# Row order through DRAM: how a four-layer graph network spreads its softmax sums and exponent rows

## The chip, the cores and the metric

The kernel runs on one core of one Trainium2 chip. The metric is the device time of one execution in microseconds (us). The core has a matrix engine (PE), a vector engine (DVE), a scalar engine (ACT), GpSimd (POOL), and a queue engine (SP) that here only issues DMAs; 16 DMA engines carry them.

## The reference

32 graphs of 512 nodes with 256 channels share one 512x512 adjacency. Each graph passes four layers, each of the form `x = x + layer(relu(layernorm(x)))`:

```
L0: e = (h W1)(h W2)^T; e = leaky(e); mask by adj; softmax; relu(att @ (h W3))
L1: q = h W, 4 heads of 64;  e[i,j] = leaky(src[i] + dst[j]); mask; softmax; elu(att @ q)
L2: 4 heads of 64: softmax(mask(Q K^T / 8)) @ V, then Wo + bo, layernorm * gamma + beta
L3: as L1, with its own weights for each head
```

## The kernel before

Everything is float32. A graph is one "work"; its 512 nodes lie as 4 row blocks (`t`) on 128 partitions. The program is unrolled and has 33 turns ("slots"). In each turn an engine runs one list of steps, written out by hand, for up to three works at once: `a` enters (layer 0 and the front half of layer 1), `b` is the work before it (the back half of layer 1, then the scores of layer 2), and `c` the one before that (the back half of layer 2, then layer 3). The engines are in order and meet only at semaphores. Three sets of buffers rotate with the work's number.

Two things need a vector that lies across partitions turned into one that lies along the free axis on every partition.

**Exponent rows of the graph layers (g = 1 and 3).** ACT writes `grow` [128 partitions, 16 values] (L511). PE transposes it into PSUM (`gat_rows`, L1060), DVE copies that to `growT` [16, 128] (`gat_rows_out`, L736), and SP stores it to `r_dram` (L322), waits, and reads it back to all 128 partitions with two loads, into `qT` and `hT` (L326). DVE's weights of the graph layer, `gat_weights` (L753), read these rows. The first work's layer 1 and the last one's layer 3 get two of their four heads from PE instead.

**Inverse sums of the multi-head softmax (layer 2), in two pairs p of heads.** DVE takes the reciprocals `rinv` (`inverse_sums2`, L815). ACT spreads a pair's into [128, 512] (`inverse_columns`, L580), PE transposes that in four pieces (`inverse_spread`, L1126), and ACT copies the result out of PSUM (`inverse_out`, L588) to `kT`, which lies in the buffer `qx`. DVE multiplies the head outputs by it (`norm2`, L822). Only then can PE do the output projection `o_rows` (L972 on `wqkvo,qT`), whose result DVE takes in `o_out` (L829), the start of layer 2's own layernorm and of layer 3's.

Around the change PE's list is: head outputs of pair 0 (L1142), 24 transposes of softmax weights (L1115), the eight transposes of the inverse sums (L1126), head outputs of pair 1 (L1142), the first head of work b's layer 1 (`gat_aggregate(b, 1, 0)`, L1080), `o_rows(c, 0)`. ACT and DVE copy the transposed weights out of PSUM (L573, L806). Later, `transposed(c, 3, 0)` (L958) starts layer 3 on PE.

SP's list in a turn is: load the input of the next work (L301), spread the rows of work a's layer 1, store work c's output (L310), spread the rows of work b's layer 3. Since it is in order, each waits for those ahead of it:

```python
                spread(a, 1); store(c); spread(b, 3)
```

The entry for work b there is served in the turn in which the other engines call that work c.

Of the kernel before, what the change touches and what calls it, by code (L numbers as in the profile page):

```python
# [5 lines left out]
def gnn_stack_kernel(nc, x, adj, W1, W2, W3, gat1_W, gat1_a, Wq, bq, Wk, bk, Wv, bv, Wo, bo,  # L6
# [5 lines left out]
    f32 = mybir.dt.float32  # L12
# [5 lines left out]
    P = 128  # L18
# [8 lines left out]
    SETS = 3  # L27
# [8 lines left out]
    with ctx:  # L36
# [47 lines left out]
        growT = sets("growT", [H * NT, P])  # L84
# [11 lines left out]
        r_dram = {g: [nc.dram_tensor(f"r_dram{g}_{s}", [H * NT, P], f32).ap() for s in range(SETS)] for g in (1, 3)}  # L96
        prob2 = [[pA[s], pB[s], pX[0], pX[1]] for s in range(SETS)]
# [12 lines left out]
        def sem(name):  # L110
# [102 lines left out]
        rT_ready = per_gat("rT_ready")  # L213
        rT_out = per_gat("rT_out")
# [32 lines left out]
        invc_ready = Signal("invc_ready", 2)  # L247
        invp_ready = Signal("invp_ready", 2)
        inv_ready = Signal("inv_ready", 2)
# [46 lines left out]
        def _(sp):  # L296
# [19 lines left out]
            def spread(w, g):  # L316
# [4 lines left out]
                rT_out[g].wait(sp, w)  # L321
                sp.dma_start(rows_dram, growT[s][:, :]).then_inc(r_written[g].sem, 16)  # L322
# [116 lines left out]
        def _(act):  # L439
# [135 lines left out]
            def inverse_columns(w, p):  # L575

                if w is None:
                    return
                rinv2.wait(act, w, p + 1)
                nc.scalar.copy(kT[w.s][:, p, :].rearrange("p (t h d) -> p t h d", t=NT, h=2),  # L580
                               rinv[w.s][:, 2 * p:2 * p + 2, :].rearrange("p h t -> p t h").unsqueeze(3)
                               .broadcast_to([P, NT, 2, D])).then_inc(invc_ready.sem, 1)

            def inverse_out(w, p):
                if w is None:
                    return
                invp_ready.wait(act, w, p + 1)
                nc.scalar.copy(kT[w.s][:, p, :], ps[:, BANK[f"RB{p}"], :]).then_inc(inv_ready.sem, 1)  # L588
# [39 lines left out]
        def _(dve):  # L628
# [103 lines left out]
            def gat_rows_out(w, g):  # L732
                if w is None:
                    return
                rT_ready[g].wait(dve, w)
                nc.vector.tensor_copy(growT[w.s][:, :], ps[0:H * NT, BANK[f"RT{g}"], 0:P]).then_inc(rT_out[g].sem, 1)  # L736

# [79 lines left out]
            def norm2(w, p):  # L817
# [3 lines left out]
                inv_ready.wait(dve, w, p + 1)  # L821
# [19 lines left out]
            def slot(a, b, c, d):  # L841
                statistics(a, 0); inverse_sums2(c, 1); weights_out2(c, 2, 3); weights_out2(c, 3, 0)
                weights_out2(c, 3, 2); mean_and_variance(a, 0); gat_weights(b, 1, 0, 0, 1, 2, 3)
                norm2(c, 0); gat_weights(b, 1, 1, 0); shift_of_norm(a, 0); norm2(c, 1)
                gat_weights(b, 1, 1, 1, 2, 3); gat_weights(b, 1, 2, 0, 1, 2); o_out(c); statistics(c, "in")
# [7 lines left out]
                inverse_sum0(a); gat_shift(c, 3); weights_out0(a, 3); gat_rows_out(c, 3); statistics(a, 1)  # L853
# [11 lines left out]
                weights_out2(b, 0, 1); gat_shift(a, 1); gat_weights(c, 3, 3, 0, 1, 2); gat_rows_out(a, 1)  # L865
# [85 lines left out]
        def _(pe):  # L951
# [104 lines left out]
            def gat_rows(w, g):  # L1056
                if w is None:
                    return
# [3 lines left out]
                if lone(w, g) is None:  # L1062
                    return
# [244 lines left out]
```

## Time and profile before

| | |
|---|---|
| median of 3 runs | 2944.5 us (2943.93 to 2946.85) |
| profiled execution, span from first to last instruction | 2943.7 us (no time of its own is listed for it beside the span) |
| PE busy | 2887.3 us, 98% |
| DVE, ACT, POOL busy | 72%, 57%, 28% |
| mean granted PE clock | 0.997 |
| DMA | 109.89 MB, mean 37 GB/s |

The span is one profiled execution; it stands 0.8 us under the median. Busy time of PE is the union of its matmuls, whose ends are modelled, so 98% says that it is hardly ever without one in flight, not that it runs at its peak. In code and rows L is the line of the kernel before.

### The profile page before, as it was taken

The numbers are of one execution on the slowest core, as the hardware profiler recorded it, in microseconds if no ns is written. First come the engines' busy times: TensorE is split into PE (matmuls) and PEld (weight loads), VectorE is DVE, ScalarE is ACT, GpSimd is POOL, SyncE is SP. The second block draws the span as 40 slices with busy tenths as digits, with TensorE's granted clock in tenths as the row PEclk, the third lists the DMA queues.
The fourth block names the chain that finished last, engine by engine and source line by source line (L and its number), as shares of the span: only waits on it lengthen the run. The fifth ranks groups of instructions, "written<-read, shape, count | busy, mean of one in ns | idle before, by whom it ended". The sixth has DMA issues, their size and how long they took to land.

```text
span 2943.7 us, 68275 instructions
## 1 busy us (share of the span) xinstructions
PE 2887.3 (98%) x27732; PEld 2034.8 (69%) x27732; DVE 2127.5 (72%) x5596; ACT 1682.3 (57%) x3554; POOL 827.8 (28%) x917
## 2 busy tenths in 40 slices
PE   7899999999999999999999999999999999999998
PEld 5566767666767666767667767667767667776766
DVE  5576787776787776877776877776877777877764
ACT  2555655655656655656655656656656656656543
POOL 2123222323222323222233232233222233222221
PEclk9999999999999999999999999999999999999999
DMA  3001011101011101011101011101011111011010
GB/s 102 22 23 45 27 41 45 44 23 45 23 44 45 44 23 44 23 44 44 38 30 44 23 45 44 37 30 44 23 45 44 34 33 40 28 37 37 17 36 30
DMA packets 58840, 109.89 MB, mean 37 GB/s; under 512 B 5568, under 2 KB 41408, under 8 KB 58528
## 3 DMA queue, kind: packets, MB, share of 16 engines
q1 hardware_dynamic: 58032, 104.61, 10.8%
q8 instruction: 220, 3.60, 0.5%
q0 software_dynamic: 496, 0.92, 0.3%
q14 instruction: 92, 0.75, 0.1%
HBM read 88.21 MB, written 17.30 MB: 36 GB/s over the span
## 4 chain that ended last, share of the span: by engine, by line
PE 77%; DVE 12%; POOL 6%; issue 2%; ACT 1%; SPq 0%; DMA 0%; POOLq 0%; DVEq 0%; ACTq 0%
PE ps L972 19%; PE ps L1080 11%; PE ps L1106 8%; PE ps L1115 8%; PE ps L978 8%; PE ps L1142 8%; PE ps L1029 8%; PE ps L958 4%; DVE stats L641 3%; POOL rstd L367 3%; POOL xc L417 3%; DVE pB L753 2%; PE ps L1017 2%; DVE nb L658 1%; DVE hn L829 1%
## 5 line engine op out<-in xcount | busy, mean ns | idle before, releaser
L389 POOL TENSOR_TENSOR qx<-qx,xc 128x512 f32<-128x512 f32 x128 | 163.7, 1279 | 869.4 <-ACT qx L529 869.4
L641 DVE BATCH_NORM_STATS2 stats<-xc 128x6 f32<-128x256 f32 x384 | 134.7, 413 | 328.6 <-POOL xc L399 264.1
L448 ACT ACTIVATE hn<-xc,nb,rstd 128x256 f32<-128x256 f32 x384 | 209.1, 592 | 163.9 <-DVE nb L658 160.7
L1080 PEld LDWEIGHTS ps<-vals,pA 128*64 128x64 f32 x8192 | 253.9, 138 | 54.6 <-issue 54.5
L972 PE MATMUL ps<-wgat,hT 128*128 128x264 f32 x1024 | 267.4, 395 | 1.8 <-ACT hT L457 1.8
L1080 PE MATMUL ps<-vals,pA 128*64 128x65 f32 x8192 | 266.4, 223 | 2.1 <-DVE pA L753 2.0
L1080 PE MATMUL ps<-vals,pB 128*64 128x65 f32 x8192 | 264.0, 223 | 0.3 <-DVE pB L753 0.2
L1080 PEld LDWEIGHTS ps<-vals,pB 128*64 128x64 f32 x8192 | 249.7, 138 | 16.8 <-issue 16.7
L457 ACT COPY hT<-ps 128x1024 f32<-128x1024 f32 x128 | 129.7, 1013 | 224.0 <-PE ps L958 219.8
L1106 PE MATMUL ps<-qx,qT 64*128 64x512 f32 x1024 | 249.8, 614 | 1.1 <-DVE hn L767 0.8
L364 POOL TENSOR_SCALAR rstd<-mv 128x4 f32<-128x4 f32 x160 | 75.0, 469 | 610.2 <-DVE mv L650 610.2
L1029 PE MATMUL ps<-vals,pB 128*128 128x256 f32 x1024 | 243.2, 381 | 1.1 <-ACT vals L469 1.1
L1142 PE MATMUL ps<-pX,vals 128*64 128x512 f32 x512 | 233.6, 599 | 2.3 <-DVE pA L806 2.3
L978 PE MATMUL ps<-hT,wqkvo 128*128 128x512 f32 x512 | 233.0, 598 | 0.8 <-ACT hT L457 0.8
L1008 PE MATMUL ps<-hT,qT 128*128 128x512 f32 x512 | 228.3, 599 | 1.1 <-ACT qT L463 1.1
L1029 PEld LDWEIGHTS ps<-vals,pB 128*128 128x128 f32 x1024 | 190.6, 191 | 38.9 <-issue 14.8
L972 PEld LDWEIGHTS ps<-wgat,hT 128*128 128x128 f32 x1024 | 179.5, 190 | 50.4 <-issue 24.9
L958 PE MATMUL ps<-ident,hn 128*128 128x128 f32 x1024 | 199.0, 280 | 11.9 <-ACT hn L448 11.1
L958 PEld LDWEIGHTS ps<-ident,hn 128*128 128x128 f32 x1024 | 132.3, 141 | 105.3 <-DVE rowmax L667 32.7
L367 POOL TENSOR_TENSOR rstd<-rstd,minus_half 128x4 f32<-128x4 f32 x160 | 192.5, 1203 | 13.3
L753 DVE SCALAR_TENSOR_TENSOR pA<-qT,gval,adjT 128x512 f32<-128x512 f32 x248 | 184.5, 785 | 6.7 <-DMA hT<-r_dram 6.5
L562 ACT ACTIVATE pX<-pX,negmax 128x512 f32<-128x512 f32 x256 | 183.4, 720 | 0.6 <-DVE negmax L797 0.6
(147 smaller groups left out, 6194.3 us busy)
## 6 DMA issues: line engine op xcount, KB each, us to landing
qT<-r_dram SPq DMA_DIRECT2D x64, 512.0 KB, 3.9
hT<-r_dram SPq DMA_DIRECT2D x64, 512.0 KB, 4.9
x_in<-in_x SPq DMA_DIRECT2D x32, 512.0 KB, 3.9
out_x<-xc SPq DMA_DIRECT2D x32, 512.0 KB, 3.0
pX<-in_adj SPq DMA_DIRECT2D x1, 1024.0 KB, 8.1
r_dram<-growT SPq DMA_DIRECT2D x64, 8.0 KB, 1.3
pX<-in_L_gnn_W SPq DMA_DIRECT2D x2, 256.0 KB, 5.2
pA<-in_L_gnn_a POOLq DMA_DIRECT2D x8, 64.0 KB, 8.8
```

Source lines behind the costliest of these rows:

```text
L367: nc.gpsimd.tensor_tensor(rstd[s][:, :], rstd[s][:, :], minus_half[:, :], ALU.pow).then_inc(rstd_ready[norm].sem, 1)
L641: last = nc.vector.bn_stats(stats[s][:, t, :], src[:, t, :])
L753: last = nc.vector.scalar_tensor_tensor(out=gat_p[s][h % 2][:, t, :], in0=row, scalar=gval[s][:, 1, t, h:h + 1], in1=adjT[:, t, :], op0=AL ...
L958: last = nc.tensor.transpose(ps[:, bank + k, t * P:(t + 1) * P], hn[s][:, t, k * P:(k + 1) * P], ident[:, :])
L972: last = nc.tensor.matmul(at, src[w.s][:, k, t * P:(t + 1) * P], wt[:, k, 0:width], start=(k == 0), stop=(k == KT - 1))
L978: last = nc.tensor.matmul(ps[:, bank + m, :], wt[:, k, m * P:(m + 1) * P], hT[w.s][:, k, :], start=(k == 0), stop=(k == KT - 1))
L1008: last = nc.tensor.matmul(ps[:, BANK[f"E{t}"], :], qT[s][:, k, t * P:(t + 1) * P], hT[s][:, k, :], start=(k == 0), stop=(k == KT - 1))
L1029: last = nc.tensor.matmul(rows_in(BANK["A"])[:, t, :], pB[s][:, t, j * P:(j + 1) * P], vals[s][:, j, 0:C], start=(j == 0), stop=(j == NT - 1))
L1080: last = nc.tensor.matmul(ps[lo:hi, BANK[f"G{g}.{h}"], t * DV:(t + 1) * DV], gat_p[s][h % 2][:, j, t * P + lo:t * P + hi], vals[s][:, j, h ...
L1106: last = nc.tensor.matmul(ps[:, BANK[f"S{p}.{t}"] + hh, :], qT[s][at, p, t * P:(t + 1) * P], kT[s][at, p, :], start=True, stop=True)
L1115: last = nc.tensor.transpose(ps[:, BANK[f"PT{h}.{t}"], j * P:(j + 1) * P], prob2[w.s][h][:, t, j * P:(j + 1) * P], ident[:, :])
L1142: last = nc.tensor.matmul(ps[hh * D:(hh + 1) * D, BANK[f"G2.{p}"], :], vals[s][:, j, h * D:(h + 1) * D], probT2[s][h][:, :, j * P:(j + 1) ...
```

## The change

Both vectors now go to DRAM directly from their partition layout. The destination is written in row order: for each of the 128 partitions its 16 values (`grow`) or 8 values (one pair of `rinv`) go to addresses that lie 128 elements apart. The access pattern's last dimension is therefore one element of 4 bytes. They are read back spread: the exponent rows as before, the inverse sums of one pair in two loads of 64 partitions each. The transposes for them on PE, the copies on ACT (L580, L588) and DVE (L736), one PSUM wait of PE (`rT_out`) and `growT` go. SP's list gets two new steps in each turn, and on DVE the second `norm2` stands one `gat_weights` instruction later.

```diff
+        inv_dram = [nc.dram_tensor(f"inv_dram_{s}", [2, 2 * NT, P], f32).ap() for s in range(SETS)]
...
-                rT_out[g].wait(sp, w)
-                sp.dma_start(rows_dram, growT[s][:, :]).then_inc(r_written[g].sem, 16)
+                grow_ready[g].wait(sp, w)
+                sp.dma_start(rows_dram.rearrange("m p -> p m"), grow[s][:, :, :].rearrange("p h t -> p (h t)"),
+                             allow_slow_non_contiguous=True).then_inc(r_written[g].sem, 16)
                 r_written[g].wait(sp, w, 16)
...
+            def inverse_spread(w, p):
+
+                if w is None:
+                    return
+                s, rows_dram = w.s, inv_dram[w.s][p]
+                rinv2.wait(sp, w, p + 1)
+                sp.dma_start(rows_dram.rearrange("m p -> p m"),
+                             rinv[s][:, 2 * p:2 * p + 2, :].rearrange("p h t -> p (h t)"),
+                             allow_slow_non_contiguous=True).then_inc(inv_written[p].sem, 16)
+                inv_written[p].wait(sp, w, 16)
+                for hh in range(2):
+                    src = rows_dram.rearrange("(o h t) p -> o h (t p)", o=1, h=2)[:, hh, :]
+                    sp.dma_start(kT[s][hh * D:(hh + 1) * D, p, :],
+                                 src.broadcast_to([D, N])).then_inc(inv_loaded[p].sem, 16)
...
-                spread(a, 1); store(c); spread(b, 3)
+                inverse_spread(b, 0); spread(a, 1); store(c); inverse_spread(b, 1); spread(b, 3)
...
-                inv_ready.wait(dve, w, p + 1)
+                inv_loaded[p].wait(dve, w, 32)
...
-                norm2(c, 0); gat_weights(b, 1, 1, 0); shift_of_norm(a, 0); norm2(c, 1)
-                gat_weights(b, 1, 1, 1, 2, 3); gat_weights(b, 1, 2, 0, 1, 2); o_out(c); statistics(c, "in")
+                norm2(c, 0); gat_weights(b, 1, 1, 0); shift_of_norm(a, 0); gat_weights(b, 1, 1, 1)
+                norm2(c, 1); gat_weights(b, 1, 1, 2, 3); gat_weights(b, 1, 2, 0, 1, 2); o_out(c); statistics(c, "in")
...
-                pT2_act[2].wait(pe, c, 2); weights_transposed2(c, 3, 3); inverse_spread(c, 0)
-                pT2_dve[2].wait(pe, c, 2); inverse_spread(c, 1); aggregate2(c, 1); gat_aggregate(b, 1, 0)
+                pT2_act[2].wait(pe, c, 2); weights_transposed2(c, 3, 3)
+                pT2_dve[2].wait(pe, c, 2); aggregate2(c, 1); gat_aggregate(b, 1, 0)
```

SP's DMAs in one turn, before. The first `r_dram` is the rows of layer 1 and the second those of layer 3; each is followed by its two loads.

```order
L301 DMA x_in<-in_x 128x4x256
L322 DMA r_dram_2<-growT 16x128
L326 DMA qT<-r_dram_2 128x1024
L326 DMA hT<-r_dram_2 128x1024
L310 DMA out_x<-xc 128x4x256
L322 DMA r_dram_1<-growT 16x128
L326 DMA qT<-r_dram_1 128x1024
L326 DMA hT<-r_dram_1 128x1024
```

The same turn on SP after the change, with the changed kernel's line numbers.

```order
L298 DMA x_in<-in_x 128x4x256
L332 DMA inv_dram<-rinv 128x8x1
L338 DMA qx<-inv_dram 64x512 x2
L319 DMA r_dram_2<-grow 128x16x1
L324 DMA qT<-r_dram_2 128x1024
L324 DMA hT<-r_dram_2 128x1024
L307 DMA out_x<-xc 128x4x256
L332 DMA inv_dram<-rinv 128x8x1
L338 DMA qx<-inv_dram 64x512 x2
L319 DMA r_dram_1<-grow 128x16x1
L324 DMA qT<-r_dram_1 128x1024
L324 DMA hT<-r_dram_1 128x1024
```

The store and the two loads of the first pair of inverse sums now stand ahead of layer 1's rows, and those of the second pair behind the output's store. Both kinds of store have one-element rows (x1).

On PE, the place between the head outputs of the two pairs, before.

```order
L1142 MATMUL ps<-pX,vals 64x512
L1142 MATMUL ps<-pA,vals 64x512
L1115 MATMUL ps<-ident,pX 128x128 x24
L1126 MATMUL ps<-ident,qx 128x128 x8
L1142 MATMUL ps<-pB,vals 64x512
L1142 MATMUL ps<-pX,vals 64x512
```

And after.

```order
L1120 MATMUL ps<-pX,vals 64x512
L1120 MATMUL ps<-pA,vals 64x512
L1103 MATMUL ps<-ident,pX 128x128 x24
L1120 MATMUL ps<-pB,vals 64x512
L1120 MATMUL ps<-pX,vals 64x512
```

The eight transposes of the inverse sums are gone, so that the head outputs of pair 1 stand directly behind the last transposes of the weights that they use.

On DVE, the two `norm2` (they write `qT` from `ps` and `qx`) among work b's `gat_weights`, before.

```order
L753 SCALAR_TENSOR_TENSOR pA<-qT,gval,adjT 128x512 x4
L822 TENSOR_TENSOR qT<-ps,qx 128x512
L753 SCALAR_TENSOR_TENSOR pB<-qT,gval,adjT 128x512
L658 SCALAR_TENSOR_TENSOR nb<-mv,rstd 128x4
L822 TENSOR_TENSOR qT<-ps,qx 128x512
L753 SCALAR_TENSOR_TENSOR pB<-qT,gval,adjT 128x512 x3
```

And after.

```order
L745 SCALAR_TENSOR_TENSOR pA<-qT,gval,adjT 128x512 x4
L814 TENSOR_TENSOR qT<-ps,qx 128x512
L745 SCALAR_TENSOR_TENSOR pB<-qT,gval,adjT 128x512
L656 SCALAR_TENSOR_TENSOR nb<-mv,rstd 128x4
L745 SCALAR_TENSOR_TENSOR pB<-qT,gval,adjT 128x512
L814 TENSOR_TENSOR qT<-ps,qx 128x512
```

The second `norm2` stands behind one more `gat_weights` instruction.

## Rows read from the trace of the kernel before

**Rows 1.** The page: the chain that ended last, share of the span by engine.

```profile
PE 77%; DVE 12%; POOL 6%; issue 2%; ACT 1%; SPq 0%; DMA 0%; POOLq 0%; DVEq 0%; ACTq 0%
```

**Rows 2.** One turn's two stretches: busy PE, PEld, DVE, ACT, POOL; granted clock, DMA.

```profile
1413.80:1484.50 70.70, 70.58 (x634) 51.06 (x634) 50.72 (x134) 44.95 (x99) 17.45 (x21) 1.00 0.13 46
1484.50:1502.50 18.00, 17.71 (x223) 10.96 (x222) 15.25 (x41) 7.56 (x13) 8.21 (x7) 1.00 0.01 2
```

**Rows 3.** Timeline of PE: start, length, operation; in brackets idle before, releaser.

```profile
1413.82 0.41 PE L958 MATMUL ps<-ident,hn 128*128 128x128 f32 x2 [0.28 <-ACT hn L448]
...
1480.15 1.13 PE L972 MATMUL ps<-wqkvo,qT 128*128 128x256 f32 x4
...
1502.50 0.41 PE L958 MATMUL ps<-ident,hn 128*128 128x128 f32 x2 [0.29 <-ACT hn L448]
```

**Rows 4.** The chain that ended last, pieces in order of time.

```profile
1463.35 0.11 PE ps L1060
...
1470.78 2.77 PE ps L1115 x24
1473.55 0.44 PE ps L1126 x4
```

**Rows 5.** Timeline around the transposes of the inverse sums, ACT and PE.

```profile
1472.77 0.59 ACT L573 COPY pX<-ps 128x512 f32<-128x512 f32 x1 [0.34 <-PE ps L1115]
...
1473.77 0.59 ACT L573 COPY pX<-ps 128x512 f32<-128x512 f32 x1
...
1474.70 0.61 PE L1142 MATMUL ps<-pB,vals 128*64 128x512 f32 x1
```

**Rows 6.** Timeline of DVE, from the inverse sums of pair 1 to `o_out`.

```profile
1472.07 0.18 DVE L815 RECIPROCAL rinv<-rowsum 128x8 f32<-128x8 f32 x1
...
1474.37 2.70 DVE L753 SCALAR_TENSOR_TENSOR pA<-qT,gval,adjT 128x512 f32<-128x512 f32 x4
1476.99 0.68 DVE L822 TENSOR_TENSOR qT<-ps,qx 128x512 f32<-128x512 f32 x1
...
1478.39 0.69 DVE L822 TENSOR_TENSOR qT<-ps,qx 128x512 f32<-128x512 f32 x1
1479.00 2.07 DVE L753 SCALAR_TENSOR_TENSOR pB<-qT,gval,adjT 128x512 f32<-128x512 f32 x3
...
1484.57 1.23 DVE L829 TENSOR_TENSOR hn<-ps,b_rows 128x1024 f32<-128x1024 f32 x1 [1.52 <-PE ps L972]
```

**Rows 7.** Timeline of SP's DMA issues, layer 3's rows, then layer 1's and the output's store.

```profile
1428.19 0.32 SPq L322 DMA_DIRECT2D r_dram<-growT  x1
1429.55 0.32 SPq L326 DMA_DIRECT2D qT<-r_dram  x1
1429.91 0.43 SPq L326 DMA_DIRECT2D hT<-r_dram  x1
...
1463.81 0.32 SPq L322 DMA_DIRECT2D r_dram<-growT  x1
1465.66 0.32 SPq L326 DMA_DIRECT2D qT<-r_dram  x1
...
1470.87 0.39 SPq L310 DMA_DIRECT2D out_x<-xc  x1
```

**Rows 8.** Timeline: the inverse sums of pair 0 and the exponent rows.

```profile
1460.33 0.18 DVE L815 RECIPROCAL rinv<-rowsum 128x8 f32<-128x8 f32 x1
...
1462.14 0.24 ACT L511 ACTIVATE grow<-gexp 128x16 f32<-128x16 f32 x1
```

**Rows 9.** DMA issues: count, KB each, median us to landing; page, then 1462 to 1476 us.

```profile
hT<-r_dram SPq DMA_DIRECT2D x64, 512.0 KB, 4.9
out_x<-xc SPq DMA_DIRECT2D x32, 512.0 KB, 3.0
...
hT<-r_dram SPq DMA_DIRECT2D x1, 512.0 KB, 6.5
```

**Rows 10.** DMA packets in 10.3 to 10.8 us, while the small weight blocks load.

```profile
DMA packets 482, 0.14 MB, mean 283 GB/s; under 512 B 453, under 2 KB 482, under 8 KB 482
```

More of the change, by code:

```diff
@@ L83, in gnn_stack_kernel @@
         grow = sets("grow", [P, H, NT])
-        growT = sets("growT", [H * NT, P])
         pX = [sb(f"pX{n}", [P, NT, N]) for n in range(3)]
@@ L246, in gnn_stack_kernel @@
         rinv2 = Signal("rinv2", 2)
-        invc_ready = Signal("invc_ready", 2)
-        invp_ready = Signal("invp_ready", 2)
-        inv_ready = Signal("inv_ready", 2)
+        inv_written = [Signal(f"inv_written{p}", 16) for p in range(2)]
+        inv_loaded = [Signal(f"inv_loaded{p}", 32) for p in range(2)]
         agg2_ready = Signal("agg2_ready", 2)
@@ L573, in weights_out2 @@
                 nc.scalar.copy(probT2[w.s][h][:, t, :], ps[:, BANK[f"PT{h}.{t}"], :]).then_inc(pT2_act[h].sem, 1)
[L575 to L588, printed above, removed]
             def slot(a, b, c, d):
-                inverse_columns(c, 0); exp2(c, 3, 3); gat_exp(b, 1); weights_out2(c, 2, 2)
-                weights_out2(c, 3, 1); inverse_columns(c, 1); weights_out2(c, 3, 3); inverse_out(c, 0)
-                inverse_out(c, 1); normalised(a, 0, 0); normalised(a, 0, 1); normalised(a, 0, 2)
+                exp2(c, 3, 3); gat_exp(b, 1); weights_out2(c, 2, 2)
+                weights_out2(c, 3, 1); weights_out2(c, 3, 3)
+                normalised(a, 0, 0); normalised(a, 0, 1); normalised(a, 0, 2)
                 normalised(a, 0, 3); h_transposed(a, 0); normalised(c, "in", 0); normalised(c, "in", 1)
@@ L730, in gat_shift @@
                                         ALU.mult, ALU.min).then_inc(gexp_ready[g].sem, 1)
[L732 to L736, printed above, removed]
             def gat_weights(w, g, h, *ts):
@@ L864, in slot @@
                 gat_norm(c, 3, 1); gat_max(a, 1); weights_out2(b, 1, 0); inverse_sums2(b, 0)
-                weights_out2(b, 0, 1); gat_shift(a, 1); gat_weights(c, 3, 3, 0, 1, 2); gat_rows_out(a, 1)
+                weights_out2(b, 0, 1); gat_shift(a, 1); gat_weights(c, 3, 3, 0, 1, 2)
                 gat_weights(c, 3, 3, 3); weights_out2(b, 0, 3); weights_out2(b, 2, 1); weights_out2(b, 1, 2)
@@ L943, in first @@
                 mean_and_variance(a, 1); shift_of_norm(a, 1); poison(); adjacency_out(); gat_max_t(a, 1)
-                gat_max(a, 1); gat_shift(a, 1); gat_rows_out(a, 1)
+                gat_max(a, 1); gat_shift(a, 1)
                 dve.wait_ge(setup_ok, SETUP)
@@ L1056, in gat_rows @@
             def gat_rows(w, g):
-                if w is None:
+                if w is None or lone(w, g) is None:
                     return
                 grow_ready[g].wait(pe, w)
-                nc.tensor.transpose(ps[0:H * NT, BANK[f"RT{g}"], 0:P], grow[w.s][:, :, :].rearrange("p h t -> p (h t)"),
-                                    ident[:, :]).then_inc(rT_ready[g].sem, 1)
-                if lone(w, g) is None:
-                    return
                 for h in range(2):
@@ L1117, in weights_transposed2 @@
                 last.then_inc(pT2p_ready[h].sem, 1)
-            def inverse_spread(w, p):
-                if w is None:
-                    return
-                invc_ready.wait(pe, w, p + 1)
-                for t in range(NT):
-                    cols = slice(t * P, (t + 1) * P)
-                    last = nc.tensor.transpose(ps[:, BANK[f"RB{p}"], cols], kT[w.s][:, p, cols], ident[:, :])
-                last.then_inc(invp_ready.sem, 1)
             def aggregate2(w, p):
@@ L1192, in slot @@
                 agg0_norm.wait(pe, a, 4); v_rows(b, 2, 0); scores2(b, 0, 0); scores2(b, 1, 0)
-                rT_out[3].wait(pe, c); scores2(b, 0, 1)
+                scores2(b, 0, 1)
                 masked2[0].wait(pe, b, 2); scores2(b, 0, 2); v_rows(b, 2, 1)
```

4 lines of the change are left out of this document (1 added, 3 removed), and 4 rows, old and new, of the table BANK.

## The prediction

> **What bounds the kernel now.** The chain that ended last comes first: 77% of it is PE, and DVE and POOL have 18% [rows 1]. So PE is the bound for most of the span but not for all of it, and one must ask where. The stretches show it: a turn is 88.7 us long, 70.7 us of it from the first transpose of layer 3 (L958) to the end of the output projection, and 18.0 us from there to the same transpose of the next turn [rows 2]. At the end of the second stretch PE sits idle for 0.28 us until ACT delivers `hn`, in this turn and in the next [rows 3]: those 18.0 us are a chain from `o_out` over two layernorms on DVE, POOL and ACT, and PE's work in it is cover. In the 70.7 us PE works without a break. A microsecond taken from PE in the first stretch moves `o_rows` and everything behind it; nothing that the change touches lies in the second. All 88.7 us turns are alike, and 32 of the 33 have the steps that the change touches, so I work in times of the turn around 1413.8 to 1502.5 us and multiply by 32. The sum is made against the span of 2943.7 us; the median of the runs is 0.8 us above it, and I put the difference on the median.
>
> **What the change takes from PE.** The transpose of the exponent rows costs PE 0.11 us, twice in a turn (L1060, the one at 1463.35 stands for both) [rows 4]. Both stand in the first stretch, with PE work ready behind them: 0.22 us.
>
> The eight transposes of the inverse sums begin at 1473.55 [rows 4] and the head outputs of pair 1 (L1142) at 1474.70 [rows 5], so they take 1.15 us. But this is not what goes. L1142 needs the last block of weights, which PE has transposed by 1473.55 and which ACT copies from 1473.77 to 1474.36 [rows 5]. Today the eight transposes hide that copy. Without them ACT, which no longer has L580 ahead, starts it as it started the one before: that block was complete after 16 of the 24 transposes, at 1470.78 + 16 x 0.115 = 1472.63, and ACT began at 1472.77, 0.14 us later [rows 4, 5]. So the copy runs from 1473.69 to 1474.28, and with about 0.12 us for the semaphore PE starts at 1474.40, 0.30 us earlier than now. PE will stand idle there for 0.85 us of the 1.15. The sum is 0.22 + 0.30 = 0.52 us in a turn, and 32 x 0.52 = 16.6 us.
>
> The copies taken from ACT (L580, L588) and DVE (L736) lie beside other work and give nothing more. On DVE the second `norm2` ran from 1478.39 to 1479.07 [rows 6]; one `gat_weights` (2.07 / 3, 0.67 us between starts) later and some 0.2 us earlier through PE's lead it ends at about 1479.5. PE reaches `o_rows` at 1480.15 - 0.52 = 1479.63 [rows 3]. This just fits, with 0.1 us to spare. Behind it DVE waits 1.52 us for `o_out` anyway [rows 6].
>
> **What it adds: one-element rows.** The store of exponent rows becomes 128 x 16 = 2048 pieces of 4 bytes, 128 for each of the 16 DMA engines; that of a pair of inverse sums 1024 pieces, 64 for each. Today's store has one piece for each engine, and the load that waits for it is issued 1.36 us after it [rows 7]. The price e of one such piece is shown nowhere. From below it is nothing. From above, a general bound: the output's store has 32 pieces of 1 KB for each engine and lands in 3.0 us [rows 9], (3.0 - 1.33) / 31 = 54 ns. The nearest row is that of the weight blocks: 482 packets, 453 of them under 512 bytes, in 0.5 us on 16 engines [rows 10], 30 for each engine, which is 16.6 ns a packet, in a stretch in which the engines had work throughout. Those were 256-byte loads. A 4-byte piece has less to move but the same fixed part, so I take e = 12 ns. A store with n pieces for each engine then takes 1.33 us + n e from its issue to the load's issue: 2.9 us for the exponent rows, 2.1 us for a pair of sums.
>
> The Trainium skill ("DMA: Bandwidth & Descriptors", "Rules for kernel authors") says that a strided last dimension lowers to one descriptor per element and advises against it. The same page ("Specifications") says that below 512 bytes the DMA engine does a read-modify-write. For the loads of [rows 10] the trace shows no such penalty; for stores of 4 bytes no row here can show it. By that rule e would be the third rival's below.
>
> **Where the new steps wait.** SP is in order, so I follow it.
> - Pair 0: the sums are there at 1460.51 [rows 8]. Store at 1460.6, its loads at 1461.93 + 0.064 e, SP free again 0.72 us later (two issues, 0.36 us apart as in [rows 7]) at 1462.65 + 0.064 e, e in ns. The exponent rows have been there since 1462.38 [rows 8]; before, SP got them at 1463.81 over PE and DVE [rows 7].
> - Exponent rows of layer 1: the two small loads ahead in the DMA engines cost some 0.6 us (an estimate, 256 KB at half the time of the 512 KB load's data), so the big loads go out at 1464.6 + 0.192 e. With e = 12 that is 1466.9, against 1465.66 today [rows 7], 1.2 us later. `hT` is issued 0.36 us behind and lands after 4.9 us in the median and 6.5 in this turn [rows 9]: 1472.2 to 1473.8. DVE reads it at 1474.37 [rows 6], or 0.2 us earlier. It stays hidden, for e up to 14 in the worst turns and 21 in the median.
> - Output's store: free to go at 1470.87 as today [rows 7], its data behind what is left of the big loads.
> - Pair 1: sums at 1472.25 [rows 6]. Its store is queued in the DMA engines behind the output's. The data of the big loads end about 0.7 us before they land, the output's data need 1.6 us, the pieces 0.064 e, 0.25 us for SP, then two loads of 64 x 2 KB. Their landing lies between 1.33 us and the 3.0 us of the output's 512 KB; I take 2.6, and 0.36 for the second issue. With 0.7 us of `norm2` and its semaphore, `o_rows` can start at 1475.7 + 0.256 e in an average turn (0.8 later in this one). With e = 12 that is 1478.8, against the 1479.63 at which PE comes.
> - Layer 3's rows: their store also skips the hop over PE and DVE, which for layer 1 took 1463.81 - 1462.38 = 1.4 us, and pays 128 e = 1.5 us. The loads go out when they do now.
>
> So the gain is whole up to e = 15, zero at e = 17.4 (`o_rows` at 1480.15), and each nanosecond above costs 0.256 x 32 = 8.2 us. What waits behind it: on SP layer 3's rows, on DVE the rest of work b's `gat_weights`, on PE everything.
>
> **Forecast: 2944.5 - 16.6 = 2928 us**, and 2918 to 2937 for this case alone (0.8 us of gain at most, 0.25 at least).
>
> **Rivals.**
> 1. *The pieces are as slow as big ones; slower.* With e = 30 `o_rows` starts at 1483.4, 3.2 us late: 2944.5 + 104 = 3049. With the bound of 54 it starts at 1489.5: +300, 3245. It decides at e = 17.4, only 5 ns above my value. For it: nothing shows a 4-byte store, and 16.6 ns would already take all the gain. Against it: packets got cheaper with size wherever rows show both. Chance 0.29 with all values of e from 18.5 up, without the next.
> 2. *No change.* e between 16 and 18.5, or `norm2`, one instruction later, taking the gain with its 0.1 us of room. 2940 to 2950, chance 0.11.
> 3. *Each piece is a read and a write.* As a mechanism of this kernel: each store piece costs two small packets, 2 x 16.6 = 33 ns, `o_rows` at 1484.2, 4.0 x 32 = +128: 3072. Chance 0.10. This is the read-modify-write of the Trainium skill's page named above.
> 4. *All 1.15 us go.* If the last copy were not awaited, 1.37 us a turn and 2901 us. Against it speaks the copy's end at 1474.36, and DVE's `norm2` at 1479.5, which then binds. Chance 0.03.
>
> The forecast's own case keeps 0.47. A measurement of this kernel tells about 0.2% (6 us) from no change. Faster: 0.47 + 0.03 = 0.50; same 0.11; slower 0.39. Range: 2918 leaves out rival 4; the upper end of 3110 is e = 37 and leaves out the part above, about 0.17.
>
> **What would show it.** Right: L1060 and L1126 gone, PE idle for some 0.85 us ahead of L1142, the turn 88.2 us, `norm2` without a wait for a DMA, the stores landing in 2 to 3 us. Wrong: DVE L822 or L753 released by DMAs from `inv_dram` or `r_dram`, a gap on PE in front of `o_rows`, stores of more than 3.6 us. If PE's gaps grow the granted clock may fall as well, which I do not price.

## The result, and the profile after

| | before | after |
|---|---|---|
| median | 2944.3 us (2943.93 to 2946.85, 4 runs) | 3829.1 us (3827.78 to 3830.52, 4 runs) |
| span of the profiled execution | 2943.7 us | 3827.3 us |
| mean granted PE clock | 0.997 | 0.903 |
| packets under 512 bytes | 5,568 | 205,249 |

The ratio is 1.300, with a 95% interval of 1.298 to 1.302. The median is far outside the range of 2918 to 3110, and on the other side of the forecast. The extra 885 us are spread over all turns: the one that I followed is 116.6 us long instead of 88.7, and 32 times these 27.9 us are 893.

The page of the changed kernel: busy time of each engine, granted clock in 40 slices, packets, and the chain that ended last by engine and by line.

```profile
PE 3087.2 (81%) x27412; PEld 2169.4 (57%) x27412; DVE 2106.7 (55%) x5532; ACT 1621.1 (42%) x3426; POOL 795.4 (21%) x917
...
PEclk9898898998888998988998988988899988899988
...
DMA packets 265687, 126.91 MB, mean 33 GB/s; under 512 B 205249, under 2 KB 240065, under 8 KB 265377
...
DMA 42%; PE 26%; DVE 16%; issue 6%; POOL 5%; SPq 3%; ACT 2%; POOLq 0%; DVEq 0%; ACTq 0%
DMA r_dram<-grow 17%; DMA inv_dram<-rinv 17%; PE ps L964 14%; DMA hT<-r_dram 5%; PE ps L1094 4%; PE ps L950 3%; DMA qx<-inv_dram 3%; DVE pB L745 2%; DVE pA L745 2%; POOL rstd L380 2%; DVE stats L639 2%; POOL xc L430 2%; PE ps L1021 2%; DVE pX L779 2%; PE ps L1068 2%
```

Where PE had 77% of the chain [rows 1], DMAs have 42% now, and the two new kinds of store alone 34%. PE waits for what hangs behind them. The waits of PE, then those of SP: what was waited for, us in total, times, longest. "issue" is time in which the engine waited for nothing that the profile shows.

```profile
PE ps L1068 <- DVE pA L745: 287.5, 34, 14.5
PE ps L964 <- DVE qT L814: 198.7, 32, 8.3
PE ps L1068 <- issue: 89.6, 57, 4.6
PE ps L1094 <- DVE rowmax L779: 78.7, 31, 4.4
...
SPq L324 <- DMA r_dram<-grow: 629.4, 64, 10.9
SPq L338 <- DMA inv_dram<-rinv: 616.6, 56, 14.5
```

SP waits 629.4 / 64 = 9.8 us for a store of rows and 616.6 / 56 = 11.0 us for one of sums. Its timeline through one turn shows the order: pair 0's sums, work a's rows, the output, pair 1's sums.

```profile
1884.01 0.37 SPq L332 DMA_DIRECT2D inv_dram<-rinv  x1
1893.57 1.10 SPq L338 DMA_DIRECT2D qx<-inv_dram  x2
1894.71 0.59 SPq L319 DMA_DIRECT2D r_dram<-grow  x1
1904.15 0.34 SPq L324 DMA_DIRECT2D qT<-r_dram  x1
...
1905.01 0.43 SPq L307 DMA_DIRECT2D out_x<-xc  x1
1905.49 0.61 SPq L332 DMA_DIRECT2D inv_dram<-rinv  x1
1919.52 1.09 SPq L338 DMA_DIRECT2D qx<-inv_dram  x2
```

From a store's issue to the next issue it takes 9.56 us for pair 0, 9.44 for the rows and 14.03 for pair 1, which has the output's store ahead of it. I had 2.1 and 2.9 for the first two. The load for the rows leaves 1904.15 - 1884.01 = 20.1 us after pair 0's store, instead of 1466.9 - 1460.6 = 6.3. Who waits at the end, on DVE and then on PE:

```profile
1911.59 2.74 DVE L745 SCALAR_TENSOR_TENSOR pA<-qT,gval,adjT 128x512 f32<-128x512 f32 x4 [8.83 <-DMA hT<-r_dram]
...
1923.34 0.69 DVE L814 TENSOR_TENSOR qT<-ps,qx 128x512 f32<-128x512 f32 x1 [7.02 <-DMA qx<-inv_dram]
...
1914.47 3.72 PE L1068 MATMUL ps<-vals,pA 128*64 128x65 f32 x64 [8.09 <-DVE pA L745]
1924.09 2.07 PE L964 MATMUL ps<-wqkvo,qT 128*128 128x256 f32 x4 [5.89 <-DVE qT L814]
```

Work b's weights wait 8.83 us for the rows, `norm2` of pair 1 waits 7.02 us for its sums, and PE stands 8.09 and then 5.89 us. In this turn the 64 matmuls behind the first wait take 3.72 us; 64 of the same form take 2.09 us at 1937.18, where PE had not stopped. The windows view of a later turn shows the clock behind such a wait at 0.67, a mixture of its two levels, 1.2 and 2.4 GHz (busy times, clock, DMA share, GB/s):

```profile
2031.00:2041.00 10.00, 3.46 (x64) 3.35 (x64) 2.21 (x5) 2.08 (x4) 0.00 (x0) 0.67 0.14 28
```

The rows of layer 3 are late in the same way. Their store is issued at 1847.50 and the loads behind it at 1857.85, 10.35 us later instead of 1.36 [rows 7], and DVE waits for them:

```profile
1863.17 0.75 DVE L745 SCALAR_TENSOR_TENSOR pA<-qT,gval,adjT 128x512 f32<-128x512 f32 x1 [3.34 <-DMA hT<-r_dram]
```

DVE's row maxima of work b (`rowmax`) stand behind these weights in its list, and PE's 78.7 us are the wait for them.

What takes the 10 us is not the pieces. The DMA view of 1848 to 1858 us, in 40 slices of 0.25 us, shows one store of rows that was issued at 1847.50, and nothing else but 16 packets (the first row is the busy share of the 16 DMA engines in tenths):

```profile
DMA  0077776000000000000000000000000000000000
...
DMA packets 2064, 0.01 MB, mean 1 GB/s; under 512 B 2064, under 2 KB 2064, under 8 KB 2064
```

The 2048 pieces pass within five slices, 1.25 us, or 1.25 / 128 = 9.8 ns for each on an engine. I had put e at 12 ns. They are gone at 1849.75, the load that waits for them is issued at 1857.85, and in those 8.1 us no packet of any DMA passes. One piece for each element is what the Trainium skill says of a strided last dimension ("DMA: Bandwidth & Descriptors", "Rules for kernel authors"); the 2,064 packets agree. The same page ("Anatomy of one DMA") says, of DMAs that GpSimd issues, that the fixed part is mostly the receipt of the last write, and that it can be surprisingly long into HBM; it has about 2 us. The 8.1 us of this trace, on SP's queue, lie in the same place, behind the last piece; that they are such a receipt no row shows.

### The profile page after: what moved, and what is told of

The parts are those of the page before. It is cut to its first block, busy times and chain, and to the rows that moved or that the text cites. A ratio compares the mean times of both kernels' runs of the same rounds, so it can differ in the third digit from the quotient of the medians.

```text
span 3827.3 us, 67603 instructions
## 1 busy us (share of the span) xinstructions
PE 3087.2 (81%) x27412; PEld 2169.4 (57%) x27412; DVE 2106.7 (55%) x5532; ACT 1621.1 (42%) x3426; POOL 795.4 (21%) x917
## 2 busy tenths in 40 slices
DMA packets 265687, 126.91 MB, mean 33 GB/s; under 512 B 205249, under 2 KB 240065, under 8 KB 265377
## 4 chain that ended last, share of the span: by engine, by line
DMA 42%; PE 26%; DVE 16%; issue 6%; POOL 5%; SPq 3%; ACT 2%; POOLq 0%; DVEq 0%; ACTq 0%
DMA r_dram<-grow 17%; DMA inv_dram<-rinv 17%; PE ps L964 14%; DMA hT<-r_dram 5%; PE ps L1094 4%; PE ps L950 3%; DMA qx<-inv_dram 3%; DVE pB L745 2%; DVE pA L745 2%; POOL rstd L380 2%; DVE stats L639 2%; POOL xc L430 2%; PE ps L1021 2%; DVE pX L779 2%; PE ps L1068 2%
## 5 line engine op out<-in xcount | busy, mean ns | idle before, releaser
L1068 PE MATMUL ps<-vals,pA 128*64 128x65 f32 x8192 | 317.5, 246 | 287.5 <-DVE pA L745 287.5
L1068 PEld LDWEIGHTS ps<-vals,pA 128*64 128x64 f32 x8192 | 299.6, 159 | 349.0 <-issue 348.1
L1068 PE MATMUL ps<-vals,pB 128*64 128x65 f32 x8192 | 295.7, 228 | 91.3 <-issue 89.6
L964 PE MATMUL ps<-wqkvo,qT 128*128 128x256 f32 x512 | 197.8, 529 | 198.7 <-DVE qT L814 198.7
L1068 PEld LDWEIGHTS ps<-vals,pB 128*64 128x64 f32 x8192 | 272.1, 142 | 115.6 <-issue 113.6
L1094 PE MATMUL ps<-qx,qT 64*128 64x512 f32 x1024 | 267.4, 640 | 79.7 <-DVE rowmax L779 78.7
L377 POOL TENSOR_SCALAR rstd<-mv 128x4 f32<-128x4 f32 x160 | 52.8, 330 | 1262.8 <-DVE mv L648 1262.8
L1120 PE MATMUL ps<-pX,vals 128*64 128x512 f32 x512 | 255.0, 644 | 2.2 <-ACT pA L586 1.7
L964 PEld LDWEIGHTS ps<-wqkvo,qT 128*128 128x128 f32 x512 | 127.7, 275 | 222.6 <-DVE qT L814 205.1
L461 ACT ACTIVATE hn<-x_in,nb,rstd 128x256 f32<-128x256 f32 x128 | 66.4, 589 | 435.3 <-DVE nb L656 435.3
```

What stands on the lines that cost most here:

```text
L461: nc.scalar.activation(hn[s][:, t, :], src[:, t, :], ACT.Identity if norm == "in" else ACT.Relu, bias=nb[s][:, t:t + 1], scale=rstd[s][:, ...
L964: last = nc.tensor.matmul(at, src[w.s][:, k, t * P:(t + 1) * P], wt[:, k, 0:width], start=(k == 0), stop=(k == KT - 1))
L1068: last = nc.tensor.matmul(ps[lo:hi, BANK[f"G{g}.{h}"], t * DV:(t + 1) * DV], gat_p[s][h % 2][:, j, t * P + lo:t * P + hi], vals[s][:, j, h ...
L1094: last = nc.tensor.matmul(ps[:, BANK[f"S{p}.{t}"] + hh, :], qT[s][at, p, t * P:(t + 1) * P], kT[s][at, p, :], start=True, stop=True)
L1120: last = nc.tensor.matmul(ps[hh * D:(hh + 1) * D, BANK[f"G2.{p}"], :], vals[s][:, j, h * D:(h + 1) * D], probT2[s][h][:, :, j * P:(j + 1) ...
```

## The experiments

All are compared with the kernel before, whose median was 2945.1 to 2946.0 us beside them. The first four divide the change.

**Rows alone.** The kernel before, with only the exponent rows stored in pieces:

```diff
-                rT_out[g].wait(sp, w)
-                sp.dma_start(rows_dram, growT[s][:, :]).then_inc(r_written[g].sem, 16)
+                grow_ready[g].wait(sp, w)
+                sp.dma_start(rows_dram.rearrange("m p -> p m"), grow[s][:, :, :].rearrange("p h t -> p (h t)"),
+                             allow_slow_non_contiguous=True).then_inc(r_written[g].sem, 16)
```

> One part alone: only the exponent rows go to DRAM in 4-byte pieces; the inverse sums keep the kernel before's path over ACT and PE. In the changed kernel such a store takes 9.4 to 10.4 us from its issue to the issue of the load behind it, against 1.36. Theory A (the stores' long completion is what costs, each where it is awaited): layer 3's rows come about 7.9 us later less the 1.4 us hop, DVE waits some 3.5 us; layer 1's come 6.5 us later against 1.9 of slack, 4.6 us; together with PE's slower clock behind the gaps 8 to 12 us a turn, so 3200 to 3330 us. Rival (the two parts only hurt together, because SP is in order and the pair-0 step stands ahead of the rows): under 3 us a turn, below 3040 us.

**Sums alone.** The changed kernel, with the rows over PE and DVE again (that diff the other way round) and one semaphore `inv_written` for both pairs.

> The other part alone: only the inverse sums go to DRAM in 4-byte pieces, in the order of the changed kernel on SP; the exponent rows keep the path over PE. Theory A: SP waits 9.6 us for pair 0 (1460.6 to 1470.2 in the turn of the kernel before), layer 1's rows are stored then instead of at 1463.81, 6.4 us late against a slack of 1.9 to 3.5 us; pair 1 is stored behind the output and completes 14 us after its issue, so o_rows starts some 8 to 13 us late: 12 to 16 us a turn in all, 3330 to 3460 us. If this and the run with the rows alone add up to the 885 us of the whole change, the parts are independent; if they add to clearly less, they hurt more together. Rival as there: under 3 us a turn.

Measured: 3284.8 us for the rows alone (ratio 1.1145, 1.1123 to 1.1167), 3472.9 us for the sums alone (1.1784, 1.1766 to 1.1802). That is +340 and +528, together 868, where the whole change has +885. So neither half needs the other to cost. The first lies in its expected range, the second 13 us above it. PE's waits, of the rows alone and then of the sums alone:

```profile
PE ps L1105 <- DVE rowmax L788: 103.9, 31, 4.4
PE ps L1079 <- issue: 57.5, 91, 2.8
```

```profile
PE ps L972 <- DVE qT L822: 258.8, 32, 9.4
PE ps L1080 <- issue: 86.6, 43, 3.4
```

Each half has its own wait and also one that is released by nothing ("issue"). With the rows alone PE's longest wait in sum is the one behind layer 3's rows (`rowmax`, 103.9 us), with the sums alone the one behind `norm2`.

**Wide pieces.** The changed kernel, with both stores in the order of the partitions, 64 or 32 bytes in a piece; every instruction and wait stays. It leaves out the turn into row order, so that rows and sums come back permuted and the kernel computes something else in the same steps.

```diff
-                sp.dma_start(rows_dram.rearrange("m p -> p m"), grow[s]...
+                sp.dma_start(rows_dram.rearrange("m p -> (m p)").rearrange("(p m) -> p m", p=P), grow[s]...
```

> The changed kernel with both stores written in partition order, so that each partition's 16 or 8 values are one piece of 64 or 32 bytes; they are read back in the wrong order, so the values of rows and sums are permuted, and all instructions, waits and queues are those of the change. Theory A: the stores complete in about 1.5 us, nothing waits for them, and only the gain of the prediction is left, 0.52 us a turn: 2928 us (2920 to 2940). Rival (the cost lies in SP's order, in the loads of the sums or in the bare number of DMAs, not in the one-element pieces): stays above 3000 us.

Measured: 2934.1 us, ratio 0.9960 (0.9947 to 0.9972). All 895 us between the two are thus the layout of the two stores. The page (KB each, median us to landing) and PE's timeline ahead of pair 1:

```profile
PE 2847.4 (97%) x27412; PEld 2003.3 (68%) x27412; DVE 2110.8 (72%) x5532; ACT 1620.3 (55%) x3426; POOL 826.6 (28%) x917
...
r_dram<-grow SPq DMA_DIRECT2D x64, 8.0 KB, 2.0
inv_dram<-rinv SPq DMA_DIRECT2D x64, 4.0 KB, 1.7
```

```profile
1465.46 0.61 PE L1120 MATMUL ps<-pB,vals 128*64 128x512 f32 x1 [0.88 <-ACT pX L586]
```

The stores land in 2.0 and 1.7 us, and PE waits 0.88 us for ACT's last copy. Against this kernel, which has the same instructions, the 894.9 us of the changed one's span divide: PE is busy 3087.2 - 2847.4 = 239.8 us longer with the same 27,412 matmuls (the clock), and idle 655.1 us longer. The four rows of its waits above sum to 654.5, and the same four come to 3.8 us in all with wide pieces.

**The probe.** The kernel before, with two tests and a marker store in each turn, in SP's idle stretch behind the input's load. Nobody reads them, and SP alone waits for them, one after another, so that its waits price each form.

```diff
+            sp.dma_start(dst, src, allow_slow_non_contiguous=True).then_inc(probe_sem, 16)
+            probes[0] += 16
+            sp.wait_ge(probe_sem, probes[0])
...
+        PROBES = [("vals_sixteen", "load"), ("vals_eight", "apart_sixteen"), ("vals_four", "apart_row"),
+                  ("vals_one", "apart_two"), ("major", "apart_four"), ("gap", "apart_eight"),
+                  ("pair", "sbuf"), ("oct", "wide")]
```

> The kernel before, plus stores that nobody reads: in each turn, in SP's idle stretch behind the input's load, two test DMAs from a constant tile and a plain marker (16 pieces of 512 bytes), each awaited by SP alone, so that the next issue shows how long it took. 16 forms. Row order with 16, 8, 4 and 1 values for each partition; 16 values with neighbouring partitions 2, 4, 8, 16 and 128 elements apart in DRAM; partition order in pieces of 64 bytes, 4 bytes with gaps, 512 bytes; pieces of 8 and 32 bytes in row order; one-element pieces into SBUF; a one-element load. Theory A1 (pieces that fall into the same 64 bytes of DRAM wait for each other, 16 x 0.5 us): row order 9.5 us whatever the number of values, 5.5, 3.5 and 2.5 us at 2, 4 and 8 apart, 2.7 us at 16 and 128 apart, 8 bytes wide 5.3 us, 32 bytes wide 2 us. Theory A2 (any store of pieces below 64 bytes has one fixed tail of 8 us): 9 to 10 us for every form with 4-byte pieces into DRAM, wherever they fall. Theory A3 (each piece costs its engine a fixed time): 9.5 us for 16 values, 5 for 8, 1.8 for 1. For all of them SBUF as the target is 2 to 3 us. If PE's instruction supply suffers from such stores, PE shows gaps of 1 us and more released by nothing also here, although no engine waits for a store; if not, the whole stays at 2944.

**The probe, second place.** In the first place the input's load, a few microseconds earlier, still ran ahead of the test. So the kinds that had stood there stood second, behind a small marker store.

> The probe again, with the marker first and each form second, so that the input's 512 KB load, which stood right ahead of the first place, no longer weighs on it. Forms: row order with 16, 8, 4 and 1 values for each partition; 16 values in partition order with gaps; 64-byte pieces; 8-byte and 32-byte pieces in row order. In the first probe the first place cost some 2 us more than the second (12.3, 11.0, 10.0, 8.2, 12.5, 3.7, 6.3 and 3.7 us in this order of forms). Theory A1 as modified by the first probe (a chain of pieces in the same 64 bytes, 0.3 to 0.45 us for each, on a base of 1.5 to 4.5 us): 10, 9, 8, 6, 10, 1.6, 4 and 1.6 us; 32-byte and 64-byte pieces cost as little as 512-byte ones although they are no longer. Rival (the load ahead is not what differs): the same times as in the first place.

The second places of both, as SP's waits (total, times, longest), the second probe first. The names end in the number of values for each partition, or in the distance of the pieces in elements of 4 bytes; `gap` has 16 values for each partition 8 bytes apart, `pair` pieces of 8 bytes, `oct` of 32, `major` of 64, `wide` of 512, and `pr` is the same source into SBUF.

```profile
SPq L205 <- DMA pdvals_sixteen<-ident: 40.4, 4, 10.6
SPq L205 <- DMA pdgap<-ident: 36.0, 4, 10.1
...
SPq L205 <- DMA pdvals_one<-ident: 26.7, 4, 6.9
SPq L205 <- DMA pdpair<-ident: 12.0, 3, 4.1
SPq L205 <- DMA pdmajor<-ident: 4.6, 4, 1.4
SPq L205 <- DMA pdoct<-ident: 4.0, 3, 1.6
```

```profile
SPq L205 <- DMA pdapart_two<-ident: 29.2, 4, 7.8
SPq L205 <- DMA pdapart_four<-ident: 21.0, 4, 5.6
SPq L205 <- DMA pdapart_sixteen<-ident: 18.8, 4, 5.5
...
SPq L205 <- DMA pdapart_eight<-ident: 17.6, 4, 4.7
...
SPq L205 <- DMA pr<-ident: 7.6, 3, 3.0
SPq L205 <- DMA pdwide<-ident: 3.6, 3, 1.2
```

Per store SP waits 10.1 us (the issue itself, some 0.4 us, is not in it) for 2048 packed pieces and still 6.7 for 128: a sixteenth of the pieces saves a third. The same 2048 pieces take 4.4 to 4.7 us where they lie 32 or 64 bytes apart, and 2.5 us in SBUF. Pieces of 32 and 64 bytes take 1.2 to 1.3 us, and those of 512 bytes 1.2. So the wait follows how closely small pieces lie together in DRAM far more than their number. Two rows say that distance is not all. At 8 bytes from piece to piece, pieces of 4 bytes take 7.3 us in row order (`apart_two`), 9.0 where the neighbours come from one partition (`gap`), and pieces of 8 bytes only 4.0 (`pair`). Of the expected theories none holds whole: A2 fails by the pieces that lie apart, A3 by the 128 pieces, and A1 has the right order of the forms, but too little for pieces 64 bytes apart (2.7 us from issue to issue, where some 5 were measured). The kernels with the probes took 2945.6 and 2943.7 us, one run each: in this place on SP the stores cost nothing that shows. The Trainium skill says that the DMA engine does a read-modify-write below 512 bytes ("DMA: Bandwidth & Descriptors", "Specifications"); at 32 and 64 bytes these rows show no penalty against 512.

**Overlapped.** The changed kernel, with SP issuing pair 0's store and the rows' store before it waits for either.

```diff
-                inverse_spread(b, 0); spread(a, 1); store(c); inverse_spread(b, 1); spread(b, 3)
+                inverse_spread(b, 0); spread(a, 1); spread_back(a, 1); inverse_back(b, 0); store(c)
+                inverse_spread(b, 1); inverse_back(b, 1); spread(b, 3); spread_back(b, 3)
```

> The changed kernel with SP's waits moved: the store of pair 0 and that of layer 1's rows are both issued before either is awaited, so that their completions run side by side; nothing else differs. Theory A (each 4-byte store has a long completion, and SP, in order, puts one behind the other): layer 1's rows are stored right when they are there instead of 9 to 10 us later, so DVE's wait for them (8.8 us in a turn of the changed kernel) falls by 3 to 6 us and the turn of 116.6 us to 110 to 114: 3620 to 3750 us. Rival (stores in flight together hold each other up and take as long as one after the other): 3800 us and more.

Measured: 3752.4 us, ratio 1.2738 (1.2720 to 1.2755), 77 us less than the changed kernel and less of a gain than expected. PE's waits and SP's:

```profile
PE ps L1079 <- issue: 131.2, 119, 4.7
PE ps L1079 <- DVE pA L756: 91.2, 33, 12.5
...
SPq L329 <- DMA r_dram<-grow: 779.0, 63, 16.7
SPq L348 <- DMA inv_dram<-rinv: 388.9, 33, 13.8
```

The wait for layer 1's rows fell from 287.5 to 91.2 us as intended, but SP's waits for the two kinds of store are still 779.0 + 388.9 = 1167.9 us, where one after the other they were 629.4 + 616.6 = 1246.0. In one turn the loads for layer 1's rows leave 1870.0 - 1853.5 = 16.5 us after pair 0's store, instead of 20.1. Side by side the two take nearly as long as in turn, and the gaps that nothing releases grew from 89.6 to 131.2 us.

**Unread.** The kernel before, with one store of 1024 packed pieces in each turn, at pair 0's place, which nobody reads and SP awaits only in the next turn. No step waits for it.

```diff
+                rinv2.wait(sp, w, 1)
+                sp.dma_start(unread_dram.rearrange("m p -> p m"), ident[:, 0:8],
+                             allow_slow_non_contiguous=True).then_inc(w12_in, 16)
...
-                spread(a, 1); store(c); spread(b, 3)
+                unread(b); spread(a, 1); store(c); spread(b, 3)
```

> The kernel before, with one extra store of 1024 4-byte pieces from a constant tile in each turn, issued where the changed kernel issues that of pair 0 (when its sums are ready, ahead of the rows of layer 1), read by nobody and awaited only a turn later. It tells apart what a 4-byte store does to others. Theory S (it holds up what comes after it in the DMA engines and the instruction supply): PE shows gaps of 1 us and more released by nothing inside the aggregations of layer 3, 2 to 3 us a turn, and the plain 512-byte store of the rows behind it completes late, 5 to 9 us after its issue instead of 1.4 to 1.9, which its slack of 1.9 to 3.5 us does not cover: 3 to 8 us a turn, 3040 to 3200 us. Rival (only those who wait for the 4-byte store pay, and PE's gaps in the changed kernel come from its own late start): 2945 us within 6.

Measured: 3077.1 us, ratio 1.0441 (1.0425 to 1.0457): +131 us for 32 stores that nobody awaits. PE's waits, SP's timeline and PE's:

```profile
PE ps L1091 <- issue: 75.6, 50, 3.3
...
1525.18 0.37 SPq L334 DMA_DIRECT2D unread<-ident  x1
1528.45 0.32 SPq L324 DMA_DIRECT2D r_dram<-growT  x1
1534.28 0.33 SPq L328 DMA_DIRECT2D qT<-r_dram  x1
...
1532.48 0.22 PE L1091 MATMUL ps<-vals,pB 128*64 128x65 f32 x1 [1.78 <-issue]
```

The plain store of the rows behind it, 512 bytes in a piece, takes 5.83 us instead of 1.36 to 1.85 [rows 7]. Over all turns SP's timeline has 5.6 to 7.7 us for it. The Trainium skill says that the semaphore's increment lands only after every earlier write of that DMA engine ("DMA: Bandwidth & Descriptors", "Queues, rings and completion order"), which agrees: the load behind the plain store leaves 9.1 us after the unread one was issued, and in the probe a store of 1024 packed pieces takes 8.8 us and its issue. And PE stops among its small matmuls (64 of them in 2.09 us, 0.03 us apart) with nothing to wait for. In 28 of the 32 turns a gap of over 0.5 us begins 5.5 to 6.6 us after the issue of the unread store.

**Unread, two controls.** The same number of stores at the same place: in the order of the partitions (pieces of 32 bytes), and with the same 1024 pieces of 4 bytes, but 64 bytes apart.

```diff
-                sp.dma_start(unread_dram.rearrange("m p -> p m"), ident[:, 0:8],
+                sp.dma_start(unread_dram.rearrange("m p -> (m p)").rearrange("(p m) -> p m", p=P), ident[:, 0:8],
```

```diff
-        unread_dram = nc.dram_tensor("unread", [8, P], f32).ap()
+        unread_dram = nc.dram_tensor("unread", [8, P, 16], f32).ap()[:, :, 0]
```

> Control of the unread store: same place, same bytes, same number of partitions, but each partition's 8 values as one 32-byte piece. Theory S (4-byte pieces in the same 64 bytes of DRAM hold up the DMA engines, and PE's instructions with them): no gaps on PE, the rows' store behind it in 1.4 to 2.5 us, 2945 us within 6. Rival (any extra store at this place does it): 3077 us again.

> The unread store with its 1024 pieces of 4 bytes 64 bytes apart, so that no two fall into the same 64 bytes; number and size of the pieces are those of the unread store. In the probe this form took 4.6 to 5.3 us with 2048 pieces, against 8.3 to 10.8 us for 1024 packed ones. If sharing 64 bytes is what holds things up: gaps on PE shrink to under half (75.6 us in all before) and the kernel takes 2945 to 2990 us. If the small size alone does it: 3050 us and more.

Measured: 2945.5 us for both, ratios 0.9998 (0.9989 to 1.0007) and 1.0001 (0.9992 to 1.0011), and PE's waits list no such gap. The plain store behind takes 1.35 to 3.7 us there. The last one's page and the unread kernel's have the same row of packets, but for the mean rate; this is the one 64 bytes apart:

```profile
DMA packets 92121, 110.03 MB, mean 37 GB/s; under 512 B 38848, under 2 KB 74688, under 8 KB 91808
```

So 92,121 packets cost nothing here and 131 us when 1024 of each turn's are packed. Neither the size nor the number of the pieces does it.

**Two hops.** The kernel before, with pair 0 and layer 3's rows off PE but without packed pieces: a store in the order of the partitions, a load of single elements that turns it, a store of 512-byte rows, the spread loads.

```diff
+                sp.dma_start(flat, src).then_inc(hop.sem, 16)
+                hop.wait(sp, w, at + 16)
+                sp.dma_start(dst[:, :], flat.rearrange("p m -> m p"),
+                             allow_slow_non_contiguous=True).then_inc(hop.sem, 16)
```

> A version without any 4-byte store: pair 0's sums and layer 3's rows, the two with the most time, go to DRAM in partition order (pieces of 32 and 64 bytes), come back as 8 or 16 rows with a one-element load (3.4 us in the probe), are stored in 512-byte rows and spread as before. Layer 1's rows and pair 1 keep PE. PE loses one transpose of rows and four of sums in a turn. Theory: every hop stays hidden (pair 0 has 16 us until its use, layer 3's rows arrive 3 us later than before against 3.7 of slack); of the wide-piece version's 0.40 us a turn some 0.2 to 0.3 remain: 2935 to 2940 us. Rival (a hop is not hidden, most likely layer 3's rows in the turns in which instruction loads interfere): 2945 to 2970 us.

Measured: 2948.9 us, ratio 1.0012 (1.0003 to 1.0020), so not the gain I expected. Its page has 172,761 packets, 115,136 of them under 512 bytes, and costs 3 us for them: single-element loads don't do what packed stores do. The time lies in the range of the expected rival, a hop that isn't hidden. A turn is 88.48 us long (88.58 before), but PE waits 14.9 us in all for ACT's copy of pair 1's sums, and the turns at both ends are longer. I didn't follow that further.

**Columns early.** The gain side of the forecast says that PE hides ACT's last copy. So I moved one step of the kernel before, on ACT, out of that copy's way:

```diff
-                weights_out2(c, 3, 1); inverse_columns(c, 1); weights_out2(c, 3, 3); inverse_out(c, 0)
+                inverse_columns(c, 1); weights_out2(c, 3, 1); weights_out2(c, 3, 3); inverse_out(c, 0)
```

> The kernel before with one step of ACT moved: inverse_columns(c, 1) stands ahead of weights_out2(c, 3, 1) instead of behind it. In the kernel before PE's last four transposes of the sums start at 1473.99, 0.12 us after that copy's end at 1473.87, and the head outputs at 1474.70. With the copy 0.8 us earlier the eight transposes run without a break into 1474.43, and the head outputs start when ACT's last copy is through, 1474.5: 0.2 us a turn, 2939 us. Rival (weights_out2(c, 3, 1), 0.15 us later, or the last copy hold PE up as much): 2945 us.

Measured: 2939.1 us, ratio 0.9977 (0.9968 to 0.9986), 6.4 us less than before (2945.57 beside it); it beats both kernels with nothing of the computation changed. ACT's timeline and PE's:

```profile
1470.78 0.62 ACT L580 COPY qx<-rinv 128x512 f32<-128x512 f32 x1
...
1472.04 0.59 ACT L573 COPY pX<-ps 128x512 f32<-128x512 f32 x1 [0.16 <-PE ps L1115]
...
1471.84 1.04 PE L1126 MATMUL ps<-ident,qx 128*128 128x128 f32 x8
1472.89 0.61 PE L1142 MATMUL ps<-pB,vals 128*64 128x512 f32 x1
```

The last copy follows the transposes by 0.16 us, and PE gets from the first transpose of the sums to pair 1 in 1.05 us instead of 1.15 [rows 4, 5]. The turn is 88.41 us long, 0.17 less than before; the remainder I can't show in rows.

## Why the prediction was wrong

**The step that failed** is "A store with n pieces for each engine takes 1.33 us + n e". It has the wrong form. The term n e was well sized: 1.25 us for the rows against 1.5 forecast. The constant, taken from a store with one 512-byte piece for each engine [rows 7], was not: for the packed rows it is 9.44 - 1.25 = 8.2 us. All rows from which I bounded the store ([rows 9] and [rows 10]) had large pieces or loads, and the upper bound of 54 ns for e, which would have given 4.8 us for a pair of sums and 8.2 for the rows, rested on the same form. The probe shows on what it depends, as SP's wait: packed 4-byte pieces 6.7 to 10.1 us, the same pieces 32 or 64 bytes apart 4.4 to 4.7, pieces of 32 bytes and more 1.2 to 1.3. Why small DRAM writes close together are confirmed late stays open; no row shows inside the memory. Several partitions in one small block are not needed for it, since `gap` has one partition's pieces there and takes 9.0 us.

**The step on SP** followed the right path. The chain pair 0, layer 1's rows, output, pair 1 is where the time went, in the order that the prediction gave: 287.5 us for `gat_weights` behind `hT`, 198.7 for `o_rows` behind `norm2`. I had `hT` hidden "for e up to 14 in the worst turns"; with two completions of some 9.5 us in a row ahead of it, it was not. Of layer 3's rows the prediction says "The loads go out when they do now"; they leave 10.35 us after the store, not 2.9, and PE's 78.7 us for `rowmax` are the price. And the terms written for pair 1 add up to 1474.7 + 0.256 e with the median landing of 4.9 us, not to 1475.7; with the measured constant neither would have been near.

**Two prices were missing.** The prediction priced what the stores make others wait for, but nothing for others that don't wait. The unread store shows two such effects, which are the first price: a later plain store takes 5.83 us, and PE has gaps that nothing releases, 75.6 us there and 89.6 in the changed kernel. These gaps fall while such a store is unconfirmed and in PE's densest run of small matmuls; the probe, which sat in another stretch, had none. That PE's own instructions arrive late is my reading of this, from the absence of any releaser and from the two controls; it isn't shown directly. One row fits it: a 16 KB packet of the DMA queue that the page calls `instruction` passes at 1531.2 us, inside the gap from 1530.70 to 1532.48. That PE waited for this packet no row shows. The second price is the clock: "which I do not price". It is 239.8 us, 27% of the loss.

**The rivals.** The first had the direction, the place and the queueing, but its 8.2 us for each nanosecond of e, and so 3049 to 3245 us, came from the failed form. The third, two packets for each piece, would have shown as 33 ns a piece; the pieces pass in 9.8 ns with one packet each, and its 3072 us is off by 757. A read and a write inside the memory, behind the packets, is not excluded by that. Even the bound of 54 ns gave only 3245. The second and fourth are excluded, the fourth by the 0.88 us wait.

**The gain side held.** With wide pieces, PE waits 0.88 us ahead of pair 1 (0.85 forecast), `norm2` isn't late (PE waits for it three times, 2.5 us in all), and the kernel takes 2934 us where I had 2928. Most turns are 88.18 us long and so gain 0.40 us instead of 0.52, and two are as long as 89.3 and 89.4. So the forecast is right for a kernel in which the two stores take 2 us, and wrong for this one.

## What to carry to other kernels

Price a store that someone waits for by the time until it is confirmed, not by its pieces, and measure that time for the very layout: here the same 2048 pieces of 4 bytes took 10.1 us packed and 4.7 apart. Don't put a store of packed 4-byte pieces to DRAM beside dense work unmeasured, even where nobody waits for it: 32 such stores cost 131 us through later stores and gaps on PE in one place, and nothing that shows in the probe's. And before counting removed PE instructions as gain, look for the copy that they hide; moving one step on ACT out of that copy's way gave 6.4 us, over half of the 11.0 that the wide pieces gave by removing the transposes altogether.

## What the runs showed of the hardware

- Behind a store of 2048 packed 4-byte pieces to DRAM the load that waits for it is issued 8.1 us after the last piece has passed, with idle DMA engines. The wait depends weakly on the number (6.7 us for 128 pieces, 10.1 for 2048) and strongly on the distance: in row order 7.3 us at 8 bytes, 5.3 at 16, 4.4 to 4.7 at 32 and 64. It depends on the size too: 4.0 us for packed pieces of 8 bytes.
- Behind such a store of 1024 pieces a plain store takes 5.6 to 7.7 us, and PE has gaps of up to 3.3 us with no releaser. With the same 1024 pieces 64 bytes apart PE has no such gap, and the plain store takes 1.35 to 3.2 us.
- Behind waits of 6 to 8 us in each turn the granted clock fell to 0.67 in the 10 us shown, and to 0.903 in the mean.
